# A two-layer graph convolution with a mixture of experts: node degrees by products of four groups at once, half of the row statistics on ScalarE, edges turned between steps, and layer 1's table copied back by pairs of blocks

## The reference

```
x  = x + gnn(layernorm(x), edges)
x  = x + moe(layernorm(x))

gcn(x, W, b):  xW = x @ W
               deg = segment_sum(edge_weight, dst) + 1
               dinv = rsqrt(deg) where deg > 0
               agg = segment_sum(dinv[src] * ew * dinv[dst] * xW[src], dst) + dinv^2 * xW
               return agg + b
gnn:           relu(gcn(relu(gcn(x, W1, b1)), W2, b2))
moe:           top 2 of 8 experts by softmax(tokens @ router_w.T), weights made to sum to 1
               out = tokens + sum_e weight_e * (gelu(tokens @ w1[e] + b1[e]) @ w2[e] + b2[e])
```

## Time and profile before

| | us |
|---|---|
| median of three runs | 4470.57 (4467.15 to 4471.99) |
| profiled execution, its own time | 4468.36 |
| span of the profile | 4466.6 |
| first gather of layer 1 issued | 234.47 after the span's start |

### The profile page before, as it was taken

How to read it: one execution, slowest core, us unless ns; L and a number is a source line. 1 busy time by engine, 2 the same in 40 slices (tenths; PEclk the granted TensorE clock), 3 DMA queues, 4 the chain that set the end, 5 groups by cost and what they waited for, 6 DMA issues and landing times.

```text
span 4466.6 us, 79360 instructions
## 1 busy us (share of the span) xinstructions
PE 3671.5 (82%) x27380; PEld 3437.6 (77%) x27381; DVE 2554.7 (57%) x8924; ACT 773.6 (17%) x2385; POOL 3036.1 (68%) x3196
## 2 busy tenths in 40 slices
PE   6856666666666666666599999999999999999999
PEld 5646666666666556656589999999999999999999
DVE  7623333232232323333268888888888888888887
ACT  1300000000000000000012222222222222222222
POOL 2167777777777777777677666666666666666663
PEclk9978888888888888888789999999999999999999
DMA  6343333333333333333433333333333333333332
GB/s 147 109 143 112 112 112 111 112 111 112 111 112 112 111 112 111 112 112 111 109 113 112 106 106 106 105 105 105 106 106 106 106 106 106 107 106 107 106 106 59
DMA packets 243150, 489.19 MB, mean 110 GB/s; under 512 B 60006, under 2 KB 141225, under 8 KB 242748
## 3 DMA queue, kind: packets, MB, share of 16 engines
q0 software_dynamic: 150528, 411.24, 32.6%
q1 hardware_dynamic: 84424, 66.74, 4.9%
q10 hardware_dynamic: 7796, 6.06, 0.5%
HBM read 445.14 MB, written 38.67 MB: 108 GB/s over the span
## 4 chain that ended last, share of the span: by engine, by line
PE 45%; POOL 32%; issue 12%; DVE 7%; DMA 3%; ACT 0%; DVEq 0%; SPq 0%; ACTq 0%; POOLq 0%
POOL msg L485 31%; PE part L840 16%; PE psH L825 12%; PE psY L834 12%; DVE sel L1137 2%; DMA msg<-ytab,srcT 2%; DVE work L1226 1%; DVE nt L1219 1%; PE psT L807 1%; PE psH L840 1%; DVE work L1261 1%; DMA ytab<-msg 1%; PE psT L815 1%; PE psY L710 1%; DVE rs L1221 1%
## 5 line engine op out<-in xcount | busy, mean ns | idle before, releaser
L485 POOL DMA_INDIRECT msg<-ytab,srcT x3136 | 2988.1, 953 | 1270.8 <-issue 894.8
L840 PE MATMUL part<-sel,msg 128*128 128x96 f32 x8384 | 1120.2, 294 | 244.0 <-DMA msg<-ytab,srcT 244.0
L840 PEld LDWEIGHTS part<-sel,msg 128*128 128x128 f32 x8384 | 1094.1, 211 | 271.2 <-DMA msg<-ytab,srcT 226.4
L825 PEld LDWEIGHTS psH<-work,wbuf 128*128 128x128 f32 x6272 | 809.6, 192 | 35.4
L1137 DVE TENSOR_SCALAR sel<-iota,relT,ewT 128x96 f32<-128x96 f32 x3136 | 835.6, 341 | 2.2 <-ACT accbuf L557 1.3
L834 PE MATMUL psY<-wbuf,work 128*128 128x256 f32 x3136 | 824.8, 386 | 0.0
L825 PE MATMUL psH<-work,wbuf 128*128 128x128 f32 x6272 | 812.4, 275 | 0.0
L606 ACT ACTIVATE work<-psH,b_s 128x128 f32<-128x128 f32 x1568 | 491.1, 364 | 1582.5 <-PE psH L825 1582.5
L1145 DVE TENSOR_TENSOR accbuf<-accbuf,part 128x192 f32 x524 | 184.8, 353 | 716.5 <-PE part L840 716.4
L834 PEld LDWEIGHTS psY<-wbuf,work 128*128 128x128 f32 x3136 | 535.9, 191 | 40.6 <-ACT work L606 0.3
L840 PE MATMUL psH<-sel,msg 128*128 128x96 f32 x2080 | 356.0, 352 | 208.0 <-DMA msg<-ytab,srcT 208.0
(11 more groups left out here) (190 smaller groups left out, 2241.0 us busy)
## 6 DMA issues: line engine op xcount, KB each, us to landing
msg<-ytab,srcT POOLq DMA_INDIRECT x3136
ytab<-xS SPq DMA_DIRECT2D x99, 128.0 KB, 1.9
ytab<-msg SPq DMA_DIRECT2D x98, 128.0 KB, 1.8
xS<-in_x SPq DMA_DIRECT2D x98, 128.0 KB
out<-res SPq DMA_DIRECT2D x98, 128.0 KB
accbuf<-in_x SPq DMA_DIRECT2D x97, 128.0 KB, 3.1
wbuf<-in_L_ffn_w ACTq DMA_DIRECT2D x2, 2048.0 KB, 14.9
wbuf<-in_dst SPq DMA_DIRECT2D x1, 588.0 KB
```

Source lines behind the costliest of these rows:

```text
L485: pool.indirect_dma_start(msg[:, r * GT + j, :], None, ytab[l], bass.IndirectOffsetOnAxis(ap=srcT[:, g * GT + j:g * GT + j + 1].bitcast(U3 ...
L825: mm = pe.matmul(psH[e % 2][:, m * P:(m + 1) * P], w1_s[:, e, k, m * P:(m + 1) * P], tokS[s.u][:, k, :], start=(k == 0), stop=(k == KD - 1))
L840: m = pe.matmul(slot[:, h * W:(h + 1) * W], msg[:, tile0 + j, h * P:(h + 1) * P], sel[:, sel0 + j, :], start=(j == 0), stop=(j == GT - 1))
```

## The change

**Products of four groups at once.** One product now takes the low digits of four groups (64 columns) against the high digits of four groups (24 columns); the numbers of use are the four diagonal pieces of the 64x24 result. A step has 8 products in place of 32. For this the low digits are stored in another order (`by_number`), in chunks of 384, 400, 384 and 400 columns, and `win` holds 64 rows. The diagonal piece is picked when a transposed quarter is copied. Every quarter now needs all five banks, so all four `window_columns` and `node_columns` stand behind the last step. `gcol` comes back through the table in HBM, in the matching order.

**Half of the statistics on ScalarE.** The even blocks stay on VectorE, one in a step, four steps late (`LAG`). For each odd block ScalarE runs two ACTIVATEs with a sum output: `means` (the mean, negated) and `squares` (the sum of squared differences).

**Edges turned between steps.** Two turns come first and then one behind each of the first 14 steps. The loads of the layer weights go behind the turns, in ScalarE's order, and ScalarE waits no more for the edges to land.

**The tables in two halves.** `tables` (up to the flag `tgeneral`) runs behind the statistics, `slots` (the rest) and the reciprocal of the layernorm scale run behind the node columns; the square root of that scale is taken ahead of the window columns.

**Copies back by pairs.** ScalarE copies two turned blocks with one instruction (L557 before). The two small DMAs by way of `dtab`, and with them the loads of the experts' weights, stand behind those copies.

```diff
@@ TensorE, the turns and the steps @@
-        for n, (a, c) in enumerate(turns):
+        def turn(n):
+            a, c = turns[n]
...
-            pe.wait_ge(s_win, c + 2)
+                pe.wait_ge(s_win, len(wbanks))
             wait(pe, s_winC, c - 1)
             for k in range(HI):
-                t = pe.transpose(psH[c % 2][0:GQ, k * LO:(k + 1) * LO], win[:, k, c * GQ:(c + 1) * GQ], ident[0:LO, 0:LO])
+                t = pe.transpose(psH[c % 2][0:GQ, k * QG * LO:(k + 1) * QG * LO], win[:, c * HI + k, :], ident[0:QG * LO, 0:QG * LO])
...
+        turn(0)
+        turn(1)
         for t in range(NS):
...
-            for r in range(SG):
-                at_col = (t % SB * SG + r) * HI
+            for u in range(SG // QG):
+                at_col = (t % SB * (SG // QG) + u) * QG * HI
                 for k in range(GT):
-                    m = pe.matmul(wbanks[t // SB][0:LO, at_col:at_col + HI], wlo[:, h, r * GT + k, :], whi[:, h, r * GT + k, :],
+
+                    lo4, hi4 = u * QG * GT + k * QG, slice(u * QG * GT + k, (u + 1) * QG * GT, GT)
+                    m = pe.matmul(wbanks[t // SB][0:QG * LO, at_col:at_col + QG * HI],
+                                  wlo[:, h, lo4:lo4 + QG, :].rearrange("p r n -> p (r n)"), whi[:, h, hi4, :],
                                   start=(k == 0), stop=(k == GT - 1))
             m.then_inc(s_wmm, 1)
+            if t + 2 < NTR:
+                turn(t + 2)
...
+        window_columns(0)
+        for c in range(1, GC):
+            window_columns(c)
+            node_columns(c - 1)
         node_columns(GC - 1).then_inc(s_cols, 1)
@@ ScalarE @@
-        act.wait_ge(s_dst, 48)
-        act.wait_ge(s_ew, 48)
-        act.wait_ge(s_src, 48)
+        act.preload_act_table(ACT.Square)
...
+        def means(i):
+            b = 2 * i + 1
+            act.wait_ge(s_x[b // XS], XS * 16)
+            wait(act, s_mean, i)
+            act.activation(unread[0], xblock(b), ACT.Copy, scale=-1.0 / D,
+                           accum_out=minus_mean[:, i:i + 1]).then_inc(s_mean, 1)
+
+        def squares(i):
+            act.wait_ge(s_mean, i + 1)
+            wait(act, s_square, i)
+            act.activation(unread[1], xblock(2 * i + 1), ACT.Square, bias=minus_mean[:, i:i + 1],
+                           accum_out=square_sum[:, i:i + 1]).then_inc(s_square, 1)
...
+            while done < t:
+                means(done)
+                if done:
+                    squares(done - 1)
+                done += 1
...
+        for b in range(0, NB, 2):
+            act.wait_ge(s_y1T, b + 2)
+            act.activation(accT[:, :, PAD + b * P:PAD + (b + 2) * P].rearrange("p k (b n) -> p k b n", b=2),
+                           y1banks[b // 2 % XS][:, :].rearrange("p (b k n) -> p k b n", b=2, k=KD), ACT.Copy).then_inc(s_y1C, 1)
@@ VectorE @@
+        def statistics(i):
+            v.wait_ge(s_x[2 * i // XS], XS * 16)
+            v.bn_stats(stats[:, i, :], xblock(2 * i)).then_inc(s_stats, 1)
+
+        LAG = 4
...
+            if t >= LAG:
+                statistics(t - LAG)
+        for i in range(NH - LAG, NH):
+            statistics(i)
...
+        v.sem_inc(s_var, 1)
+        tables()
         v.wait_ge(s_cols, 1)
         v.tensor_copy(cols[:, OH:OC], cbanks[1][0:W, 0:OC - OH]).then_inc(s_colsD, 1)
+        v.wait_ge(s_std, 1)
+        link(v.reciprocal(lnscale, lnscale))
+        slots()
```

More of the change, by code:

```diff
@@ L94, in behind @@
         return v
-    win = behind(HI * NG, LO).rearrange("l (h g) -> l h g", h=HI)
+    win = behind(QG * HI * GQ, QG * LO).rearrange("l (c s) -> l c s", s=GQ)
     ohbuf = behind(GC * OC)
@@ L148, in build @@
     loT, hiT, dstT = msgw[:, 0:NT], msgw[:, NT:2 * NT], msgw[:, 2 * NT:3 * NT]
+    NH = NB // 2
+    stats = msgw[:, 3 * NT:3 * NT + NH * 6].rearrange("p (b t) -> p b t", t=6)
+    minus_mean, square_sum = (msgw[:, 3 * NT + (6 + n) * NH:3 * NT + (7 + n) * NH] for n in range(2))
     lo_i, hi_i = loT.bitcast(I32), hiT.bitcast(I32)
@@ L180, in build @@
     yS = xS
+    unread = [t.rearrange("p (k n) -> p k n", k=KD) for t in (xS[1][:, :], b2_s[-1][:, :])]
     h1, h1T = tok, tokS[0]
@@ L531, in _ @@
+        done = 0
         for n in range(len(wbanks)):
             t = min((n + 1) * SB, NS)
-            g, groups = n * SB * SG, (t - n * SB) * SG
+            while done < t:
[3 more added lines that the diff above has]
+                done += 1
+            if n == 3:
+                act.wait_ge(s_rwt, 1)
+                act.activation(rwT[:, :, :].rearrange("p k e -> p (k e)"), psT[:, 0:KD * NEXP], ACT.Copy).then_inc(s_rwt, 1)
+                act.activation(b1_s[:, :, :].rearrange("p e k -> p (e k)"), psT[:, 32:32 + NEXP * KD], ACT.Copy).then_inc(s_rwt, 1)
+            at_s, steps = n * SB * (SG // QG), (t - n * SB) * (SG // QG)
@@ L534, in _ @@
             act.wait_ge(s_wmm, t)
-            act.activation(win[:, :, g:g + groups], wbanks[n][0:LO, 0:groups * HI].rearrange("l (g h) -> l h g", h=HI),
+            act.activation(win[:, :, at_s:at_s + steps], wbanks[n][0:QG * LO, 0:steps * QG * HI].rearrange("l (s c) -> l c s", c=QG * HI),
                            ACT.Copy).then_inc(s_win, 1)
-            if n:
-                window_columns(n - 1)
+        squares(NS - 1)
+        act.wait_ge(s_var, 1)
+        act.activation(lnscale, lnscale, ACT.Sqrt).then_inc(s_std, 1)
@@ L539, in _ @@
+        for c in range(GC):
+            act.wait_ge(s_winT, c + 1)
+            act.activation(winT[:, c * W:(c + 1) * W].rearrange("s (h l) -> s h l", h=HI),
+                           psH[c % 2][0:GQ, 0:HI * QG * LO].rearrange("s (h l) -> s h l", h=HI)[:, :, c * LO:(c + 1) * LO],
+                           ACT.Copy).then_inc(s_winC, 1)
         act.wait_ge(s_cols, 1)
@@ L1033, in tables, with slots @@
             link(v.tensor_scalar(tgeneral[:, :], plain, -1.0, 1.0, ALU.mult, ALU.add))
+            v.sem_inc(s_tables, 1)
+        def slots():
             link(v.tensor_scalar(taken, taken, plain, None, ALU.mult))
```

117 lines of the change are left out of this document (52 added, 65 removed).

## The result

The changed kernel takes 4444.42 us (median of five runs); the kernel before took 4470.53 us beside it. One of the five was slow (5380.69 us, at a mean granted clock of 0.635 in place of 0.91); the others took 4440.31 to 4444.51, their own median is 4442.92, and the ratio rests on them alone. The ratio is 0.994, with a 95% interval of 0.9924 to 0.9956: 0.4 to 0.8% faster. The profiled execution took 4444.42, its span is 4442.6. The forecast was 4428.5 in a range of 4416 to 4448. So the sign and the range held, but the gain is 26 to 28 us where 42 were forecast.

A forecast was written before the change was run, and what follows sets the result against it. The wait for GpSimd's first gather was taken to bound the end. Head, steps, node columns, scales and table put the gather 43.8 us earlier; less 2 for late instructions, 42: 4468.4 - 42 = 4426, or 4428.5 against the median, range 4416 to 4448.

The forecast's parts named there:

- The frame: Whole kernel: whatever moves GpSimd's first gather moves the end by as much; gather at 190.7 in place of 234.47.
- The head: Stretch before the steps: digits start at 16.2 in place of 20.93, as VectorE's 4.72 us wait for turned edges goes.
- I take 60: TensorE's steps: 60 ns a record for the product with 64 weight and 24 moving columns, 1.06 us a step with wait.
- steps 2 to 13: Steps that carry a turn each: TensorE sets the pace at 1.77 us, 21.2 us in all, ending at 47.0.
- the turn: Four transposes on TensorE within each of steps 2 to 13: 0.71 us a step.
- lower bound: Price of a four-group product's record on TensorE: at least 27 ns, that of the 16x6 product, or 0.5 us a step.
- the product costs more: Rival, TensorE's steps: 107 ns a record, 1.8 us a step; gain only 23 us, time 4447; chance 0.13.
- 0.78 us a pair: ScalarE's mean and squares of one block: 0.78 us, 38.2 for 49, ending at 103.2 with the bank copies.
- ScalarE is late: Rival: at 1.0 us a pair ScalarE ends at 114, 11 after TensorE; gain 31 us, time 4439; chance 0.2.
- quarters: Window and node columns on TensorE, wholly behind the steps: four quarters, 13.2 us in all, ending at 119.7.
- table: Layer 1's table, from VectorE's start at 131.3 to the first gather: 59.4 us against 63.8, the last store taking 6.
- the 2 us reserved for late instructions: Gaps on TensorE while x loads, read as late instructions: 2 us left for them, taken off the gain at the end.

The follow-up runs named there:

- experiment 3: Changed kernel with half of the four-group products loading 32 of 64 weight columns, leaving out part of the sums: 4448.2 us, ratio 0.9952.
- Experiments 2 to 4: The first of these: changed kernel with 48 moving columns in each four-group product in place of 24, 4446.53 us; experiment 3 and experiment 4 have their own lines.
- experiment 10: Changed kernel with one-group products again, plus ScalarE's small gtab DMAs and layer-weight loads behind 14 means, those reading gtab behind 30: 4459.44 us.
- 11: Changed kernel with one-group products again, plus SyncE holding 34 blocks of x until step 30 of the products: 4452.53 us.
- experiment 4: Changed kernel with all step products 32 weight columns wide and banks filled beforehand, leaving out half of the sums: 4428.27 us.
- experiment 5: Changed kernel with all 16 turns of the edges ahead of the first step: 4441.52 us, ratio 0.9937.
- experiment 9: Changed kernel with only the experts' weights waiting for the last store of layer 1's table, dtab's DMAs unmoved: 4448.2 us.

## Why the prediction came out as it did

**The frame held.** The end follows the first gather one to one: 24.3 us earlier there, 24.0 at the end, and the rule holds within some 2 us over all the kernels run (one, with the experts' weights alone held back, is 3 to 4 above). The head came out at 15.86 (forecast 16.2), step 2 on TensorE at 25.66 (25.8).

**The step that failed is "I take 60"** for a product with 64 weight columns. It is 107 ns, so steps 2 to 13 ended at 57.8 and not at 47.0, and the other 35 took 64.9 us and not 56.3: 35 x 1.71 = 59.7, 3.8 of waits at digits and small parts, the rest router transposes and hops. Together that is 19.4 us of the products' end (122.70 against 103.3). Some 3 us of it are a second term, the turn: between products it cost 2.68 - 1.71 = 0.97 us and not 0.71, 12 times 0.26. Two changes of width at the 0.13 us of experiment 3 would be just that, an estimate. By the prediction's own sign (wrong if the steps lie above 1.5 us) the steps failed. I had scaled the 86 ns of a transpose with 98 weight columns down to 64. A record of such a transpose costs half as much a weight column as one of a product: 86 / 98 is 0.88 ns, against 27 / 16 = 1.7 in the lower bound of the earlier trace rows. Scaled by its columns, that lower bound would have given 108. The rival "the product costs more" had exactly this price and 4447; I gave it 0.13. That the time lies within the range is owed to that rival, which set its upper end, and not to the forecast's own step. Its reason (98 wide ones with their tail) was not the right one. Experiments 2 to 4 show the reason: not 24 or 48 moving columns, not a fixed price, but 1.67 ns a weight column. The records of four groups load the same 1024 columns a step (16 x 64) as those of one group (64 x 16), and so save hardly any time on TensorE.

**Where the gain came from instead.** Undone one at a time, the four-group product is worth 13.3 us at the gather, the table part 5.8, the halved statistics 1.9, of 24.3; such shares need not add up, and the head (5.1 us earlier) and the loss by the turns (3.9) stand beside them. The product's share is the late instructions. I had read the old pauses rightly as instructions arriving late, and the sum drops the 20 us of old gaps but for 2, without saying how much of them were such pauses. In the kernel before they sum to 9.9 us, eleven pauses from 38.8 us on, of which the longest but one is

```profile
54.19 3.53 PE L710 MATMUL part<-sel 128*16 128x6 f32 x127 [2.41 <-issue]
```

The prediction saw them only beside the loads of x. By one run each, experiment 10 shows that the long ones move with ScalarE's small DMAs and weight loads, and 11 that the loads of x make them longer.

**ScalarE.** Taken at 0.78 us a pair, it is 0.89, as its timeline shows (each operation has a second record for reading its sum):

```profile
84.45 0.40 ACT L533 ACTIVATE xS<-accbuf 128x256 f32<-128x256 f32 x1
84.76 0.19 ACT L533 ACTIVATION_READ_ACCUMULATOR xS<-accbuf 128x1 f32 x1
84.85 0.50 ACT L539 ACTIVATE b_last<-accbuf,msg 128x256 f32<-128x256 f32 x1
85.25 0.19 ACT L539 ACTIVATION_READ_ACCUMULATOR b_last<-accbuf,msg 128x1 f32 x1
85.34 0.40 ACT L533 ACTIVATE xS<-accbuf 128x256 f32<-128x256 f32 x1
...
122.74 0.53 ACT L556 ACTIVATE wbuf<-psY 64x432 f32<-64x432 f32 x1 [3.75 <-PE psY L739]
```

It began its means at 73.59, 11 us later than forecast, since the last turn was late with the steps and gtab's DMAs took 14.8 us; and it still waited 3.75 us for TensorE. That this cost nothing is luck: the wrong price of the product hid the wrong price of the pair. Once TensorE is faster, the rival "ScalarE is late" comes true (4.00 us in experiment 4).

**Behind the steps** the terms were near: quarters 15.4 (forecast 16.4, counted from the last product), scales 10.7 (11.6), table 61.4 (59.4), of which the last store took 8.3 and not 6. Sum: 19.4 - 1.0 - 0.9 + 2.0 = 19.5, from 190.7 to 210.18; less the 2 us reserved for late instructions it is 17.5, the difference between the 41.8 forecast and the 24.3 found.

**Not costed at all** was the place of the turns: between the steps they leave TensorE waiting at the start, 3.9 us (experiment 5).

## What to carry to other kernels

Scale the price of an unseen fp32 product from a product, by the larger of its weight and moving columns, and not from a transpose; if the lower bound times the ratio of columns lands above your value, that is a warning. Packing four narrow products into one wider one saves hardly any weight-load time, but it leaves a quarter of the instructions, and that pays where other DMAs crowd the queues. Put DMAs of 4-byte pieces where nobody waits for a store or for instructions: beside the last store they cost 5.5 us, and together with weight loads and narrow products 5 us of late instructions.

## What the runs showed of the hardware

- A record of an fp32 product cost 27.3 ns with 16 weight and 6 moving columns, 53 with 32 and 24, 107 with 64 and 24, 108 with 64 and 48, 200 with 64 and 120, and 0.13 us more at each change between 32 and 64 weight columns.
- Those are the prices at the lower of TensorE's two levels (1.2 GHz). Experiment 4 shows both. Windows of that run: stretch, length, busy time of each engine, granted clock, DMA share, GB/s.

```profile
46.00:48.00 2.00, 1.67 (x36) 1.38 (x34) 2.00 (x6) 1.74 (x2) 1.71 (x2) 1.00 0.66 190
...
52.00:54.00 2.00, 1.68 (x32) 1.58 (x30) 2.00 (x6) 0.00 (x0) 1.57 (x2) 0.50 1.25 26
```

  At 1.00 the four transposes take 0.56 us and 16 records of products 0.66; at 0.50 they take 0.92 and 1.02. The clock rose between 43 and 44, after TensorE had been busy without a pause through a fill (eight records with 120 moving columns, 40.01 to 41.87) and the step behind it, and fell in 50 to 52, in steps in which it waited 0.54 us for its masks. It rose so behind three of the five fills, and not behind the last two. For the changed kernel the page prints 1.00 until about 140 us, but its four transposes take 0.92 us, and its first windows with a clock below 1.00 lie there; I read its steps as run at the lower level, whatever that column says. By the 32-wide products (less the tail, 53 ns and about 31), a step would take some 0.6 of its 1.71 us at the higher level, an estimate from these rows. How to hold that level in the steps was not tried.
- A sum output on ScalarE has a record of its own, 0.19 us, and operations with one start 0.40 and 0.49 us apart, where plain copies of the same size went back to back at 0.26.
- 256 pieces of 4 bytes beside the last store of 128 KB: the gather followed SyncE's last issue by 8.8 us (201.4 to 210.2), and by 2.3 us with the pieces and the experts' weights held back (202.3 to 204.7). With only the weights held back (experiment 9) the last store still took 8.0 us.
